# GpSimd takes the last 128 of 1024 columns of each subtraction of low probabilities, with its own work respaced and two of its additions turned into transfers

## What is computed

```python
def _L0_xattn_ref(x, cond, wq, bq, wkv, bkv, wp, bp):
    q = _qdq(x) @ _qdq(wq).T + bq
    kv = cond @ wkv.T + bkv
    k, v = jnp.split(kv, 2, axis=-1)
    ...
    attn = jax.nn.softmax(jnp.einsum('bnhd,bmhd->bhnm', q, k) * scale, axis=-1)
    o = jnp.einsum('bhnm,bmhd->bnhd', attn, v).reshape(B, N, C)
    out = _qdq(o) @ _qdq(wp).T + bp
    return out
...
x = x + _L0_xattn_ref(_layernorm(x, axis=-1), ctx_2048, ...)
x = x + _L0_ffn_ref(_layernorm(x, axis=-1), ...)
```

## Time and profile before

| | us |
|---|---|
| median of three runs | 2054.96 (2053.73 to 2057.93) |
| the profiled execution, whole | 2056.21 |
| its span in the trace | 2054.5 |
| before the loop | 0 to about 77 |
| the attention loop | about 77 to 1565 |
| range check and routing | about 1565 to 1700 |
| experts | about 1700 to 2054 |

### The profile page before, as it was taken

One profiled execution on the slowest core, in us unless ns is written; L12 is line 12 of the kernel. 1 busy time (PEld: TensorE's weight loads), 2 busy tenths in 40 slices (PEclk: granted clock), 3 DMA queues, 4 the chain that ended last, 5 costly groups with the idle time before them and its releaser, 6 DMA issues. The chain is left out here.

```text
span 2054.5 us, 59262 instructions
## 1 busy us (share of the span) xinstructions
PE 1778.5 (87%) x24267; PEld 1227.5 (60%) x24326; DVE 1764.4 (86%) x2331; ACT 1341.7 (65%) x1933; POOL 936.8 (46%) x842
## 2 busy tenths in 40 slices
PE   2789999999999999999899999999994127999996
PEld 1567676666766666776667666767762013555553
DVE  5699999999999999999999999999995594666665
ACT  5478778877877787788778877878774332332332
POOL 4132433742482447236524724561434002776776
PEclk9999999999999999999999999999996568999998
DMA  5412422352345234424432352433213344566785
GB/s 177 123 36 75 120 74 61 108 138 67 74 107 137 62 99 121 119 61 108 116 96 72 103 143 63 112 91 99 68 47 83 104 154 139 181 205 216 247 263 183
DMA packets 201967, 238.95 MB, mean 116 GB/s; under 512 B 93220, under 2 KB 134180, under 8 KB 201696
## 3 DMA queue, kind: packets, MB, share of 16 engines
q1 hardware_dynamic: 169936, 153.77, 27.1%
q0 software_dynamic: 29888, 80.79, 13.4%
q10 hardware_dynamic: 1872, 0.55, 0.1%
HBM read 130.32 MB, written 70.79 MB: 98 GB/s over the span
## 5 line engine op out<-in xcount | busy, mean ns | idle before, releaser
L871 DVE TENSOR_TENSOR a_p_low<-a_p 128x1024 f16<-128x1024 f32 (+1 forms) x896 | 1120.2, 1279 | 74.3 <-ACT a_p L701 67.1
L701 ACT ACTIVATE a_p<-ps_s 128x1024 f32<-128x1024 f32 (+1 forms) x896 | 860.7, 966 | 287.1 <-PE ps_s L498 278.9
L498 PE MATMUL ps_s<-a_q_stack,a_k_stack 96*128 96x512 f16 (+1 forms) x1664 | 512.9, 383 | 8.6 <-ACT a_p L701 8.2
L624 PE MATMUL ps_o<-a_v,a_p 128*128 128x65 f16 (+1 forms) x6656 | 447.0, 194 | 42.4 <-ACT a_o_sums L729 22.3
L624 PE MATMUL ps_o<-a_v,a_p_low 128*128 128x65 f16 (+1 forms) x6656 | 446.6, 194 | 0.1
L624 PEld LDWEIGHTS ps_o<-a_v,a_p 128*128 128x128 bf16 (+1 forms) x6656 | 350.4, 98 | 143.7 <-DVE a_p_low L871 55.6
L535 PEld LDWEIGHTS ps_p<-wkv,a_ctx 128*128 128x128 f16 x4992 | 324.9, 99 | 156.2 <-DVE a_v L886 43.3
L535 PE MATMUL ps_p<-wkv,a_ctx 128*128 128x128 f16 x4992 | 369.3, 222 | 40.4 <-DVE a_v L886 32.5
L517 PE MATMUL ps_p<-a_ctx,wkv 128*128 128x384 f16 (+2 forms) x1536 | 349.9, 334 | 0.0
L624 PEld LDWEIGHTS ps_o<-a_v,a_p_low 128*128 128x128 f16 (+1 forms) x6656 | 317.3, 98 | 0.2 <-issue 0.2
L517 PEld LDWEIGHTS ps_p<-a_ctx,wkv 128*128 128x128 f16 x1536 | 148.3, 98 | 140.2 <-issue 3.5
(11 more groups left out here) (240 smaller groups left out, 2012.2 us busy)
## 6 DMA issues: line engine op xcount, KB each, us to landing
a_k_stack<-a_k_parts SPq DMA_DIRECT2D x378, 80.0 KB, 2.1
d_ys<-f_y SPq DMA_DIRECT2D x71, 256.0 KB
a_ctx_raw<-in_ctx_dram POOLq DMA_DIRECT2D x64, 192.0 KB, 3.4
a_q_stack<-d_q_t SPq DMA_DIRECT2D x96, 128.0 KB, 3.4
a_xm<-in_x_dram SPq DMA_DIRECT2D x8, 1024.0 KB, 6.0
a_ctx_raw<-in_ctx_dram POOLq DMA_DIRECT2D x32, 256.0 KB, 4.0
d_q_t<-a_q_parts SPq DMA_DIRECT2D x32, 256.0 KB, 2.9
d_q_full<-a_xm SPq DMA_DIRECT2D x32, 256.0 KB, 2.8
```

The costliest lines, as they stand in the source:

```text
L498: mm = pe.matmul(t["ps_s"][s % 2][0:r, n * N:(n + 1) * N], t["k_stack"][v % 2][0:TERMS * DH, j, kt * P:kt * P + r], t["q_stack"][v % 2][0: ...
L624: mm = pe.matmul(t["ps_o"][:, q * VC:(q + 1) * VC], part[0:r, n * N + q * P:n * N + (q + 1) * P], val, start=(g == 0 and n == 0 and low == ...
L701: act.activation(t["p"][s % NP][0:r, 0:len(tiles) * N], t["ps_s"][s % 2][0:r, 0:len(tiles) * N], ACT.Exp, scale=float(DH) ** -0.5 / WSCALE ...
L871: dve.tensor_tensor(t["p_low"][s % NP][0:r, 0:n], full, high, ALU.subtract).then_inc(lows, 1)
```

## The change

- **The share.** `SHARE = 128`. For each of the 768 slots with two tiles VectorE subtracts 896 columns, and GpSimd the last 128 (`share_low`), as its first work of the slot, behind a wait for the exponential. TensorE waits for it (`shared`) ahead of the last matmul of the slot's values alone. The 128 slots with one tile stay whole on VectorE.
- **Normalising** is split: the addition, the multiplication and the bias stand in three slots, two apart.
- **Bias and residual.** For batches 0 to 6 the operations L1150 and L1156 and the load of `x` go. In their place GpSimd issues two accumulating transfers into `o_full` for each tile: the bias row spread over 128 partitions, 2 slots behind the projection, and the tile of `x`, 4 slots later, which waits for the first. SP stores the sum 3 slots later than before. Batch 7 keeps the old way.
- **Before the loop** the values' half of the weight is split earlier (slots 27 and 28 instead of 30 and 33), and GpSimd's first context piece waits until the first inverse deviation of the queries is done.

```diff
+SHARE = 128
...
-    "gate": dict(logits=1), "project": dict(y=1, x2=2, x2_store=8), ...
+    "gate": dict(logits=1), "project": dict(y=1, bp_add=2, x_add=6, x2_store=11), ...
...
         for v in range(UNITS):
-            self.put("normalise", v, 0, (v + 1) * SLOTS + (16 if v % NBLK == 2 else 5))
+            for step in range(3):
+                self.put("normalise", v, step, (v + 1) * SLOTS + (16 if v % NBLK == 2 else 5) + 2 * step)
...
-                        ("sx_copy", 26), ("kv_high_k", 17), ("kv_low_k", 25), ("kv_high_v", 30), ("kv_low_v", 33)):
+                        ("sx_copy", 26), ("kv_high_k", 17), ("kv_low_k", 25), ("kv_high_v", 27), ("kv_low_v", 28)):
...
+        def wait_x2(eng, b, m):
+            if b + 1 < B:
+                eng.wait_ge(x_added[m % 2], 16 * ((b * QT + m) // 2 + 1))
+            else:
+                eng.wait_ge(x2_ready, m + 1)
...
@@ def do_values(s):
                         for q in range(QT):
+                            if n == GROUP - 1 and low == 1 and q == QT - 1:
+                                pe.wait_ge(shared, s // GROUPS * (GROUPS - 1) + g + 1)
...
@@ def low_probabilities(s):
                 r, n = rows_of(tiles[-1]), len(tiles) * N
+                if len(tiles) == GROUP:
+                    n -= SHARE
...
@@ def _(pool):
+            def share_low(s):
+                if len(group_tiles(s % GROUPS)) < GROUP:
+                    return
+                pool.wait_ge(shifted, s + 1)
+                a, e = GROUP * N - SHARE, GROUP * N
+                full = t["p"][s % NP][:, a:e]
+                high = full.bitcast(BF16).rearrange("p (n two) -> p n two", two=2)[:, :, 1]
+                pool.tensor_tensor(t["p_low"][s % NP][:, a:e], full, high, ALU.subtract).then_inc(shared, 1)
...
             for s in range(FIRST, END):
                 if s == 0:
                     pool.wait_ge(rows_in, 32)
+                if 0 <= s < LAST:
+                    share_low(s)
...
                 for b, n in plan.at("context", s):
+                    if b == 0 and n == 0:
+                        pool.wait_ge(q_first_rooted, 1)
                     context_low(pool, b, n)
...
+                for b, m in plan.at("bp_add", s):
+                    wait_freed(pool, ("project", b, m))
+                    pool.dma_start(t["o_full"][b % 2][:, m, :], t["bp"][None, :].to_broadcast([P, C]),
+                                   accum_op=ALU.add).then_inc(bp_added, 16)
+                for b, m in plan.at("x_add", s):
+                    pool.wait_ge(bp_added, 16 * (b * QT + m + 1))
+                    pool.dma_start(t["o_full"][b % 2][:, m, :], token_rows(t["x"], b, m),
+                                   accum_op=ALU.add).then_inc(x_added[m % 2], 16)
```

More of the change, by code:

```diff
@@ L149, in steps_of @@
     return [width] * (TERMS * CC * (1 if kind == "k" else len(RANGE_TILES[r])))
-OUT_SLOTS = dict(load=-6, bias=-2, round=0, ints=3, flip=4, project=10, stats=24)
+OUT_SLOTS = dict(round=0, ints=3, flip=4, project=10, stats=24)
 OUT_SLOTS_END = dict(load=0, bias=4, round=0, ints=1, turn=2, stats=8)
@@ L303, in attention_pass @@
         ctx_in = [sem(f"a_ctx_in{n}") for n in range(NRAW)]
+        bp_added, x_added = sem("a_bp_added"), [sem(f"a_x_added{n}") for n in range(2)]
+        first_in, first_keys = [sem(f"a_first_in{n}") for n in range(CC)], sem("a_first_keys")
         ctx_high, ctx_split = sem("a_ctx_high"), sem("a_ctx_split")
@@ L318, in attention_pass @@
         first_split = sem("a_first_split")
-        first_in, first_keys = [sem(f"a_first_in{n}") for n in range(CC)], sem("a_first_keys")
         biases_in, rows_in, biases, gate_high, kv_in, kv_high, kv_low = (
@@ L1087, in _, with normalise @@
             out_done = Steps(pool, out_step)
-            def normalise(v):
+            out_added = {}
+            def share_low(s):
[6 more added lines that the diff above has]
+                pool.tensor_tensor(t["p_low"][s % NP][:, a:e], full, high, ALU.subtract).then_inc(shared, 1)
+            def normalise(v, step):
                 b, kb = v // NBLK, v % NBLK
@@ L1092, in normalise @@
                 heads = out.rearrange("p q (j d) -> p j q d", d=DH)
+                if step == 1:
+                    pool.wait_ge(out_step, out_added[v])
+                    pool.wait_ge(inverted, v + 1)
+                    out_done.n += 1
+                    out_added[v] = out_done.n
+                    pool.tensor_tensor(heads, heads, t["o_inv"][:, v, :, :, None].to_broadcast([P, HB, QT, DH]),
+                                       ALU.mult).then_inc(out_step, 1)
+                    return
+                if step == 2:
+                    pool.wait_ge(out_step, out_added[v])
+                    pool.tensor_tensor(out, out, t["bv_row"][:, None, kb * P:(kb + 1) * P].to_broadcast([P, QT, P]),
+                                       ALU.add).then_inc(out_ready, 1)
+                    return
                 pool.wait_ge(out_copied, HB * (v + 1))
@@ L1095, in normalise @@
                     pool.wait_ge(xn_low, QT * (b - 1))
[L1096 to L1101 removed]
+                out_done.n += 1
+                out_added[v] = out_done.n
+                pool.tensor_tensor(heads, sums[:, :, :, 0:DH], sums[:, :, :, DH:2 * DH], ALU.add).then_inc(out_step, 1)
             def inverse_std(v, rstd):
@@ L1144, in _ @@
                     inverse_std(t["var"][:, :], t["rstd"][:, :]).then_inc(rooted, 1)
[L1145 to L1146 removed]
+                for v, step in plan.at("normalise", s):
+                    normalise(v, step)
+                for b, m in plan.at("bp_add", s):
[6 more added lines that the diff above has]
+                                   accum_op=ALU.add).then_inc(x_added[m % 2], 16)
                 for b, m in plan.at("bias", s):
[L1148 to L1150 removed]
+                    pool.wait_ge(x_in[m % 2], 16 * (m // 2 + 1))
+                    pool.tensor_tensor(t["x_in"][m % 2][:, :], t["x_in"][m % 2][:, :], t["bp_row"][:, :],
                                        ALU.add).then_inc(biased, 1)
                 for b, m in plan.at("x2", s):
[L1153 removed]
                     wait_freed(pool, ("project", b, m))
[L1155 to L1156 removed]
+                    pool.wait_ge(biased, m + 1)
+                    pool.tensor_tensor(t["o_full"][b % 2][:, m, :], t["o_full"][b % 2][:, m, :], t["x_in"][m % 2][:, :],
                                        ALU.add).then_inc(x2_ready, 1)
```

29 lines of the change are left out of this document (8 added, 21 removed).

## The result

The changed kernel takes **2122.4 us** (median of four runs, 2119.6 to 2127.7) against 2056.4 for the kernel before, run beside it: a ratio of 1.0328, 95% interval 1.0308 to 1.0347, or 66 us more. The forecast was 2074, slower by 19. The profiled execution took 2123.9.

The account below looks back on a forecast made before the run. VectorE was taken to set the pace of most units, TensorE close behind. From the profiled 2056.2: - 104 + 99 - 27 - 5 + 42 + 14 = + 19, so 2075, median 2074 us; range 1985 to 2140.

Parts of the forecast that it names:

- VectorE sets the pace of most units: Loop: units average 46.6 us against 42.8 where VectorE has little else; TensorE close behind, relief worth at most 120 us.
- my case: Whole kernel: the summed terms give 2074 us, own range 2050 to 2110, chance 0.40.
- the smaller subtraction: VectorE's wide subtraction in the loop: 128 fewer columns save 0.135 us, 768 times, 104 us off.
- The share at the port: GpSimd's share keeps VectorE out 0.30 us, 0.43 of it landing, 768 times: 99 us more, bounds 0 and 230.
- Bias, residual and start: 56 GpSimd operations replaced by transfers take 27 us off VectorE; earlier weight split and wait before the loop, 5 us less.
- The context stretches: Seven stretches where GpSimd splits context: its queue takes 58 us against 48, 4 absorbed; 42 us more.
- The chains outside: Queries' chain of 13 on GpSimd, seven times: about 6 us each, 4 absorbed; 14 us more, between 0 and 35.
- Rival 2: GpSimd sets the pace in the seven stretches and queries' chains, 105 + 35 in place of 42 + 14: 2158 us; chance 0.14.
- Rival 1: Loop: GpSimd finds the gaps, VectorE's relief is real, 60 us left, 1995 us; chance 0.28.
- Rival 3: Every share stops a subtraction on VectorE, 230 in place of 99 us: 2205 us; decides from fraction 0.57; chance 0.08.
- Rival 4: Gain and loss cancel, stretches at half price and chains at none: about 2040 to 2059 us; chance 0.10.

Follow-up runs that it names:

- e3: Changed kernel without the share: VectorE subtracts all 1024 columns, transfers, spaced steps and earlier weight split stay; 2044.5 us, 0.9955 of the kernel before.
- e2: Changed kernel with VectorE on 896 columns, the other 128 subtracted by nobody and TensorE not waiting for them; 1999.3 us, 0.9734 of the kernel before.
- e6: Changed kernel, VectorE on all 1024 columns; GpSimd subtracts unread constants only outside context stretches and the slots by the queries' chain; 1.0083 of the kernel before.
- e1: Changed kernel with GpSimd's share done on constants into a tile nobody reads, TensorE not waiting for it; 2059.1 us, 1.0023 of the kernel before.
- e14: Changed kernel with the share only in the seven context stretches (168 shares), VectorE on all columns elsewhere; 1.0139 of the kernel before.
- e4: Kernel before with the share alone: normalising in one slot, bias and residual on GpSimd, weight split as before; 2178.3 us, 1.0600 of the kernel before.

## Why the prediction came out as it did

The direction held, and so did the place and kind of TensorE's new waits; that VectorE sets the pace of most units did not. The size was 66 us against 19: 2122 lies in the range of 1985 to 2140, but above my case's own 2110. The steps in turn:

- **"So VectorE sets the pace of most units"**, and with it the 104 us at which the smaller subtraction was put, is the step that failed. It was drawn from one unit of 42.8 us against a mean of 46.6, and from VectorE being busy in 94% of the loop. Both are true of averages. Piece by piece, TensorE sets the length of a good part, and in others neither engine is busy all the way. The relief was put at 104 us; it measured 45 (e3 to e2), with 98 us less of VectorE's busy time. This term alone is 59 us too good.
- **The share at the port, 99 us.** The fraction of a hold that lands on VectorE was taken from GpSimd's present, longer operations, 0.43. For shares it is 0.17 where GpSimd has room (e6) and about half in the stretches; over all 768 it is 62 ns each (1237 less e2's 1175), 48 us of VectorE's time. But e1 shows 60 us for the load as a whole, chiefly since the context pieces come late. So the term was too large by 39, and what is left of it is for the most part a thing that it did not contain: GpSimd's queue also delays others when nobody waits for the share. That the two exclude each other held. The Trainium skill ("SBUF — State Buffer", section "Who interferes with whom") says that the one who asks second is fully blocked; the rows agree on single instructions (a member of the chain at 0.89 to 1.16 in place of 0.20 us). The 230 us of a subtraction held at every share are about six times e6's measure (768 x 0.05). GpSimd pays more than VectorE: a share takes 0.99 us on average and 0.39 alone.
- **Bias, residual and start, 27 + 5 us.** VectorE's busy time fell by what was said, 31 us; the time fell by 4.5 for the transfers and by 9 with spacing and start together. The same failed step. The first exponential starts at 73.4 instead of 77.3, 3.9 us earlier, for some 5 forecast. An issue of an accumulating transfer takes GpSimd 0.90 us on average for the bias and 1.19 for `x`, not 0.56. VectorE never waits for one.
- **The context stretches, 42 us.** GpSimd's queue was put at 58 us for each, and with 4 of them absorbed a stretch at 54. It measured 57.1, with GpSimd busy in 50.5 and idle in 6.6, of which 3.9 are the 0.30 us behind each of 13 pieces. So the queue was priced well, and the 4 us that were to be absorbed were not: seven stretches are 56 us longer (334.4 and 390.3). e14 shows them alone, 52.
- **The chains outside, 14 us.** Each was put at 6 us, 4 of them absorbed. The one shown was 8 us long and stopped TensorE for 4.4; the piece grew by 5.8 on average, with 2.9 given back in the next: some 20 us net. What was missing is the second payment, the clock.

The balance: 19 + 59 (relief) - 39 (port) + 23 (companions and start) + 7 (TensorE's waits) = 69, against 66; the 69 are the distance to the kernel before on the chip of e1 to e4, 2053.5 us. Two errors of about 40 us of opposite sign, the port's and part of the relief's, cancel in it, which is luck.

On TensorE's side the two terms (42 + 14 = 56) stand against 63 from e1 to after: near, and partly by luck, as the clock's 20 us (1391 to 1411) were not in it. Rival 2, that GpSimd sets the pace where it has a second job, is the nearest in kind, and its 2158 is nearer to 2122 than my 2074. Rival 1 had the subtraction right: 1237 ns, where it asked for about 1200 and my case for 1300 to 1350. That row spoke for rival 1, and the time went the other way: a smaller mean on the engine that was thought to set the pace proved nothing on the time. Rival 3 is out by e6; its limit of 0.57 should have been 0.59, since the start's 5 us belong to what is saved (136 of 230). Rival 4, gain and loss cancel, is what e1 shows (1.0023) as long as nobody has to wait for a share. The share's shortest time was 0.39 us, not 0.44.

## What to carry to other kernels

Before pricing a relief, compare equal pieces of the loop for who is busy all the way through: 98 us taken off an engine that was busy in over nine tenths of the loop were worth 45. When part of a per-slot step moves to an in-order engine that also does long or chained work, the price is the waits behind that work, and the remedy is to leave the slots beside it out (from 3.3% slower to 1.5% faster with the same code), more than making the part smaller. A stop of some 4 us on TensorE cost more than its length here.

## What the runs showed of the hardware

- TensorE's clock: behind a stop of 4.43 us the granted clock was 0.50 over the next 3.8 us, and its busy time for the loop's matmuls ranges from 1372 us (e2) over 1388 (before) and 1411 (after) to 1427 (e4), and its busy time at the 0.50 level from 10 over 34 and 86 to 98 us.
- GpSimd, held at the port, can be passed more than once. Two shares in a context stretch took 5.08 us together, while VectorE ran five operations, three of them wide subtractions; alone a share takes 0.39:

```profile
605.16 5.08 POOL L1111 TENSOR_TENSOR a_p_low<-a_p 128x128 f16<-128x128 f32 x2
```

```profile
605.77 0.55 DVE L900 TENSOR_TENSOR a_v<-ps_p,a_v 128x384 f16<-128x384 f32 x1
606.24 2.08 DVE L885 TENSOR_TENSOR a_p_low<-a_p 128x896 f16<-128x896 f32 x2
608.24 0.74 DVE L1050 SCALAR_TENSOR_TENSOR a_xm<-ps_p,sq,a_sx_row 128x512 f32<-128x512 f32 x1
608.90 1.07 DVE L885 TENSOR_TENSOR a_p_low<-a_p 128x896 f16<-128x896 f32 x1
```

The holds on VectorE that the prediction counted are the smaller part. The share's mean of 0.99 us against 0.39 at its shortest says that GpSimd pays 0.6 us for each. VectorE pays 0.06 on average (after against e2): 0.15 in the context stretches and 0.04 elsewhere.
